# The state as stationary operand for z and n in a GRU with expert tiles

## What is computed

```python
def cell(h, x):
    gi = x @ W_ih + b_ih
    gh = h @ W_hh + b_hh
    r = sigmoid(i_r + h_r)
    z = sigmoid(i_z + h_z)
    n = tanh(i_n + r * h_n)
    return (1 - z) * n + z * h
...
y = sum over e of w[e] * ((silu(s @ W1[e].T) * (s @ W2[e].T)) @ W3[e].T)   # s: the states
x = x + y
```

## Time and profile before

| | us |
|---|---|
| median of 3 runs (1501.98 to 1507.65) | 1506.52 |
| span of the profiled execution | 1501.1 |
| TensorE matmul busy | 1409.4 (94%) |
| VectorE busy | 1043.8 (70%) |
| ScalarE busy | 896.3 (60%) |
| GpSimd busy | 415.8 (28%) |

### The profile page before, as it was taken

How to read it: one execution, slowest core, us unless ns; L and a number is a source line. 1 busy time by engine, 2 the same in 40 slices (tenths; PEclk the granted TensorE clock), 3 DMA queues, 4 the chain that set the end, 5 groups by cost and what they waited for, 6 DMA issues and landing times.

```text
span 1501.1 us, 88729 instructions
## 1 busy us (share of the span) xinstructions
PE 1409.4 (94%) x37804; PEld 1227.2 (82%) x37804; DVE 1043.8 (70%) x4116; ACT 896.3 (60%) x2319; POOL 415.8 (28%) x850
## 2 busy tenths in 40 slices
PE   2888878899999999999999999999999999998997
PEld 1888778888888888888888888888888888885664
DVE  7788887777677677777777767776777776764333
ACT  6677675555565556655556555665556655555664
POOL 1011112123322232222332223222333222326443
PEclk9999887899999999999999999999999999999999
DMA  8445413112221222212222122211222212223431
GB/s 290 124 130 140 134 45 90 40 32 40 46 39 39 46 46 40 39 39 46 40 46 40 39 46 46 41 38 40 46 40 46 40 39 47 39 40 79 60 49 16
DMA packets 99011, 88.64 MB, mean 59 GB/s; under 512 B 41407, under 2 KB 74175, under 8 KB 98624
## 3 DMA queue, kind: packets, MB, share of 16 engines
q0 software_dynamic: 17952, 33.64, 12.9%
q1 hardware_dynamic: 80672, 49.32, 11.5%
HBM read 59.12 MB, written 35.72 MB: 63 GB/s over the span
## 4 chain that ended last, share of the span: by engine, by line
PE 83%; DVE 10%; issue 3%; ACT 1%; POOL 1%; DMA 1%; SPq 0%; DVEq 0%; POOLq 0%; ACTq 0%
PE gn_bank L1366 12%; PE gz_ps L1366 12%; PE y_ps L1458 9%; PE b_ps L1388 9%; PE a_ps L1422 8%; PE b_ps L1422 8%; PE gi_ps L1388 8%; PE gr_ps L1357 6%; PE gr_ps L1351 6%; DVE wexp L1037 2%; PE tr_ps L1436 2%; PE tr_ps L1446 2%; PE tr_ps L1478 1%; DVE npre L1067 1%; DVE nmh L1073 1%
## 5 line engine op out<-in xcount | busy, mean ns | idle before, releaser
L1366 PE MATMUL gz_ps<-hlog,whh 128*128 128x32 f16 x8192 | 246.0, 177 | 6.1 <-issue 6.0
L1366 PE MATMUL gn_bank<-hlog,whh 128*128 128x32 f16 x8192 | 245.2, 177 | 2.4 <-issue 2.2
L625 POOL DMA_INDIRECT out_y<-work,mt x57 | 93.9, 1648 | 546.2 <-PE gz_ps L1366 309.6
L1366 PEld LDWEIGHTS gz_ps<-hlog,whh 128*128 128x128 f16 x8192 | 224.1, 96 | 6.9 <-issue 6.7
L1366 PEld LDWEIGHTS gn_bank<-hlog,whh 128*128 128x128 f16 x8192 | 224.2, 96 | 2.7 <-issue 2.7
L1351 PEld LDWEIGHTS gr_ps<-hlog,whh 128*128 128x128 f16 x4096 | 130.6, 96 | 53.9 <-DVE hlog L1080 32.4
L1351 PE MATMUL gr_ps<-hlog,whh 128*128 128x16 f16 x4096 | 141.9, 170 | 31.3 <-DVE hlog L1080 28.3
L1388 PE MATMUL b_ps<-xs,wih 128*128 128x64 f16 x4752 | 162.3, 197 | 3.4 <-issue 2.1
L1458 PE MATMUL y_ps<-wexp,work 128*128 x639 | 159.0, 382 | 1.9 <-ACT work L845 1.9
L1388 PEld LDWEIGHTS b_ps<-xs,wih 128*128 128x128 f16 x4752 | 153.3, 101 | 5.1 <-issue 3.5
L810 ACT ACTIVATE rs<-rpre,sc 128x64 f32<-128x64 f32 x256 | 88.0, 344 | 112.7 <-DVE rpre L1054 112.5
(11 more groups left out here) (217 smaller groups left out, 2550.3 us busy)
## 6 DMA issues: line engine op xcount, KB each, us to landing
wexp<-in_w_units SPq DMA_DIRECT2D x46, 256.0 KB, 3.8
x_raw<-in_x_feat SPq DMA_DIRECT2D x32, 256.0 KB, 3.7
out_y<-in_x_tok SPq DMA_DIRECT2D x16, 512.0 KB
h_tok<-xrow SPq DMA_DIRECT2D x32, 256.0 KB, 2.0
wexp<-in_w_hh SPq DMA_DIRECT2D x4, 768.0 KB, 6.8
wexp<-in_w_inproj SPq DMA_DIRECT2D x4, 768.0 KB, 11.8
wexp<-in_w_units SPq DMA_DIRECT2D x15, 192.0 KB, 4.5
mt<-meta SPq DMA_DIRECT2D x71, 1.0 KB, 1.7
```

The lines of the kernel that those rows point to most:

```text
L625: pool.indirect_dma_start(out=out, out_offset=bass.IndirectOffsetOnAxis(ap=mt[:, j % RING, 0:1].bitcast(I32), axis=0), in_=ysc[y_slot(j)], ...
L1366: mm = pe.matmul(dst[:, j], whh[:, i, k, m * P:(m + 1) * P], h[:, k], start=False, stop=True, skip_group_check=True)
```

## The change

For z and n the operands change places. The state of one chunk with both halves (128 x 32) is the stationary operand, and the weights stream past, 256 columns at a time: 8 blocks (4 of z, 4 of n) of 32 outputs. Four such matmuls, g = 0 to 3, use the four groups of 32 array columns and write to the four groups of 32 partitions of one bank, `zn_bank`; eight rounds (4 chunks, 2 halves of the weights) add up. So there are 32 matmuls in place of 64, z and n are finished together, and `gh_ready` counts two per step. r is made as before.

The results now lie with sequence and half on the partitions, in blocks of 32 x 32. VectorE turns each block back with a transpose of 32 x 32 (`turn`, one for n and one for z, from the bank to `n_parts` and `z_parts`), each followed by a sum over three numbers: the two halves and the bias or input part, which stands in the third place. For n that is written once in the setup; for z ScalarE writes it for each step (`place_z`), in place of the seed. The n seed goes. `hlog` has the two halves next to each other, so that its 32 columns are contiguous. The buffers `rs`, `zs`, `rh`, `nt` and `znh` go, and their operations write in place.

```diff
+    Q = 2 * B
-    GRU = "R HN R_HN N_PRE Z N_H Z_NH H_HI H_NEW H_LO".split()
+    GRU = "R N_TURNED HN R_HN N_PRE Z_TURNED Z N_H Z_NH H_HI H_NEW H_LO".split()
 ...
     def behind_n(t):
-        return 3 * t + 2
+        return 2 * t + 2
 ...
-        hlog = sb("hlog", [P, 2, K, 2, P], F16)
+        hlog = sb("hlog", [P, 2, K, P, 2], F16)
 ...
+        n_parts = sb("n_parts", [P, K, B, 3])
+        z_parts = sb("z_parts", [P, K, B, 3])
 ...
-        gn_bank = ps("gn_bank", [P, 512])
-        gn_ps = gn_bank[:, 0:K * 2 * B].rearrange("p (k a b) -> p k a b", k=K, a=2)
-        gz_ps = ps("gz_ps", [P, K, 2, B])
+        zn_bank = ps("zn_bank", [P, 512])
+        z_ps, n_ps = (zn_bank[:, i * K * 2 * B:(i + 1) * K * 2 * B].rearrange("p (k b a) -> p k b a", k=K, a=2)
+                      for i in range(2))
 ...
+            def place_z(t):
+                S.activation(z_parts[:, :, :, 2], gi_of(t, 1), ACT.Copy, scale=scale(SC_PLACE)).then_inc(z_placed, 1)
 ...
-                act.wait_ge(gru_ops, gru(t, "HN"))
-                if t + 1 < T:
-                    seed(gn_ps, bhn[:], n_seeded)
 ...
-                dve.wait_ge(gh_ready, 3 * t + 2)
-                halves(hn[:], gn_ps)
+                dve.wait_ge(gh_ready, 2 * t + 2)
+                turn(n_parts, n_ps)
+                after("N_TURNED")
+                total(hn[:], n_parts[:])
 ...
-                dve.wait_ge(gh_ready, 3 * t + 3)
-                halves(zpre[:], gz_ps)
+                turn(z_parts, z_ps)
+                dve.wait_ge(z_placed, t + 1)
+                after("Z_TURNED")
+                total(zpre[:], z_parts[:])
 ...
-                for dst, first, seeded in ((gn_ps, 2 * K, n_seeded), (gz_ps, K, z_seeded)):
-                    pe.wait_ge(seeded, t + 1)
-                    for j in range(K):
-                        m = first + j
-                        for k in range(K):
-                            for i in range(2):
-                                mm = pe.matmul(dst[:, j], whh[:, i, k, m * P:(m + 1) * P], h[:, k],
-                                               start=False, stop=True, skip_group_check=True)
-                    mm.then_inc(gh_ready, 1)
+
+                for k in range(K):
+                    for i in range(2):
+                        w = whh[:, i, k, K * P:M * P].rearrange("p (m x) -> p m x", x=P)
+                        for g in range(P // Q):
+                            mm = pe.matmul(zn_bank[g * Q:(g + 1) * Q, 0:4 * K * B], h[:, k].rearrange("p b a -> p (b a)"),
+                                           w[:, :, g * Q:(g + 1) * Q],
+                                           start=(k == 0 and i == 0), stop=(k == K - 1 and i == 1))
+                mm.then_inc(gh_ready, 1)
```

More of the change, by code:

```diff
@@ L54, in gru_moe_kernel @@
     assert GS == 8 and E == 8 and HE == 352 and TILES == 71 and FULL == 57
+    Q = 2 * B
+    assert Q == 32 and P // Q == K
     FIRST = 52
@@ L448, in h_parts @@
             g, s = divmod(t, GS)
-            return hlog[:, g % 2, :, :, s * B:(s + 1) * B]
+            return hlog[:, g % 2, :, s * B:(s + 1) * B]
         def raw_in(e, w):
@@ L903, in _ @@
             act.wait_ge(gates_open, 1)
-            seed(gr_ps, gi_of(0, 0), r_seeded)
-            seed(gn_ps, bhn[:], n_seeded)
-            seed(gz_ps, gi_of(0, 1), z_seeded)
+            seed_r(0)
+            place_z(0)
             for t in range(T):
@@ L933, in _ @@
                 if t + 1 < T and z_comes_late(t + 1):
-                    seed(gz_ps, gi_of(t + 1, 1), z_seeded)
+                    place_z(t + 1)
             take_rows(LAST)
@@ L1051, in op, with total, turn @@
                     ins.then_inc(gru_ops, 1)
[L1053 to L1057, removed]
+                def total(dst, parts):
+                    op(V.tensor_reduce(dst, parts, AX_X, ALU.add))
+                def turn(parts, rows):
+                    op(V.transpose(parts[:, :, :, 0:2], rows))
+                dve.wait_ge(gh_ready, 2 * t + 1)
+                total(rpre[:], gr_ps[:].rearrange("p k a b -> p k b a"))
                 behind_r(t)
-                dve.wait_ge(gh_ready, 3 * t + 2)
-                halves(hn[:], gn_ps)
+                dve.wait_ge(gh_ready, 2 * t + 2)
+                turn(n_parts, n_ps)
+                after("N_TURNED")
+                total(hn[:], n_parts[:])
                 dve.wait_ge(sig_r, t + 1)
                 after("HN")
-                op(V.tensor_tensor(rh[:], rs[:], hn[:], ALU.mult))
+                op(V.tensor_tensor(hn[:], rpre[:], hn[:], ALU.mult))
                 after("R_HN")
@@ L1076, in gru_step @@
                 after("N_H")
-                op(V.tensor_tensor(znh[:], zs[:], nmh[:], ALU.mult))
+                op(V.tensor_tensor(nmh[:], zpre[:], nmh[:], ALU.mult))
                 after("Z_NH")
-                for dst in (parts[:, :, 0], h_now[:, new]):
-                    op(V.tensor_tensor(dst, h_now[:, now], znh[:], ALU.add))
+                for dst in (parts[:, :, :, 0], h_now[:, new]):
+                    op(V.tensor_tensor(dst, h_now[:, now], nmh[:], ALU.add))
                 after("H_NEW")
-                op(V.tensor_tensor(parts[:, :, 1], h_now[:, new], parts[:, :, 0], ALU.subtract))
+                op(V.tensor_tensor(parts[:, :, :, 1], h_now[:, new], parts[:, :, :, 0], ALU.subtract))
             def expert_measure(e):
@@ L1265, in _ @@
             first = h_parts(2 * GS - 1)
-            chain(V.tensor_copy(first[:, :, 0], h_now[:, 0]))
-            chain(V.tensor_tensor(first[:, :, 1], h_now[:, 0], first[:, :, 0], ALU.subtract))
+            chain(V.tensor_copy(first[:, :, :, 0], h_now[:, 0]))
+            chain(V.tensor_tensor(first[:, :, :, 1], h_now[:, 0], first[:, :, :, 0], ALU.subtract))
             chain(V.tensor_scalar(scale(SC_GAP), scale(SC_PG), 2.0 ** -14, scale(SC_IH), ALU.mult, ALU.mult))
@@ L1477, in turn_rows @@
                         at = (i * K + k) * P
-                        mm = pe.transpose(tr_ps[:, at:at + P], h[:, k, i], ident[:])
+                        mm = pe.transpose(tr_ps[:, at:at + P], h[:, k, :, i], ident[:])
                 mm.then_inc(tr_mm, 1)
@@ L1481, in turn_rows @@
                     for k in range(K):
[L1482 removed]
+                        mm = pe.matmul(route_ps(g)[:, 0:2 * E], h[:, k, :, i],
                                        wg[:, k].rearrange("p e h -> p (e h)"),
@@ L1545, in _ @@
             pe.wait_ge(setup, N_CONSTS)
-            for gh in (gr_ps, gn_ps, gz_ps):
-                mm = pe.matmul(gh[:].rearrange("p k a b -> p (k a b)"), ident[:], ident[:], start=True, stop=True)
-            mm.then_inc(gates_open, 1)
+            pe.matmul(gr_ps[:].rearrange("p k a b -> p (k a b)"), ident[:], ident[:], start=True, stop=True
+                      ).then_inc(gates_open, 1)
             turn_x_exponent(0)
```

47 lines of the change are left out of this document (21 added, 26 removed).

## The result

The change makes the kernel slower: 1566.88 us (median of 4 runs, 1565.73 to 1567.64) against 1506.82 us (4 runs on the same chip), a ratio of 1.040 with a 95% interval of 1.0382 to 1.0418. The forecast was 1560 us; the terms behind it did less well than the sum, because two misses of nearly the same size cancel.

A forecast was written before the change was run, and what follows sets the result against it. TensorE was taken to bound steps 52 to 255 and the recurrence steps 0 to 51. Middle stage -13, first stage +49 and clock +18 make +54 us on 1506.5, so 1560 us, range 1506 to 1632.

The forecast's parts named there:

- The middle stage: Steps 52 to 255, mostly TensorE-bound: forecast 0.06 us shorter each over 203 steps, -13 us.
- the first stage: Steps 0 to 51, paced by the recurrence: forecast 0.95 us longer each, +49 us, plus 18 for the clock.
- the loop: Recurrence from one start of r to the next, through z, n and VectorE's chain: forecast 5.05 us against 3.98.
- two changes of mode: On TensorE between r on the full array and the column groups, and back: forecast 0.15 us each.
- place 3: Middle-stage steps whose number modulo 8 is 3: forecast length 5.05 us.
- place 7: Middle-stage steps whose number modulo 8 is 7: forecast length 5.05 us.
- place 2: Middle-stage steps whose number modulo 8 is 2, forecast to stay TensorE's: 5.58 us, TensorE's work down 0.42.
- E: End of the last z and n matmul; from there to the next r 3.08 us were forecast.
- The clock: Steps 0 to 51: streaming matmuls take about 1.7 us at the lower clock, 40% of the stage, +18 us.
- The first: Rival: cheaper turns and free mode change shorten the loop to 4.50, break even at 4.82; 1438 us, chance 0.10.
- The second: Rival: the four column groups run one after another, loop 7.66, about 2210 us; chance 0.10 together with the third.
- the third: Rival: weight loads don't hide, 8 rounds take 1.62 us, loop 5.79, about 1750 us; chance 0.10 together with the second.

The follow-up runs named there:

- e3: Changed kernel with all four matmuls of a round on the same 32 array columns, values not the reference's: 2197.6 us in one run.
- e4: Changed kernel with VectorE making the scale of hidden before the input-product batch in every fourth step: 1553.11 us, 1.029 of the kernel before.
- e5: Kernel before with one wait moved, so VectorE takes n only when z is finished too: 1531.48 us, ratio 1.0142.
- e9: Kernel before with an unread transpose ahead of each of the sums of n and z: 1527.06 us, ratio 1.0166.
- e6: Changed kernel with six unread matmuls of 512 columns a step in steps 0 to 49: 1558.51 us, 1.0322 of the kernel before.
- e7: Changed kernel with one transpose for n and z, hidden scale before input products, and the added clock-keeping matmuls: 1483.13 us, 0.9834 of the kernel before.
- e8: Kernel before with only the state's two halves laid side by side, read with doubled stride: 1507.39 us, ratio 0.9997.
- e1: Changed kernel with one transpose of 256 elements for n and z in place of two of 128: 1496.68 us, 0.9924 of the kernel before.
- e10: Changed kernel with z before n in two banks, z turned while n runs, hidden scale before input products: 1579.13 us, 1.0504 of the kernel before.
- e2: Changed kernel with n before z in two banks, 64 matmuls of 128 columns in place of 32 of 256: 1524.86 us, 1.011 of the kernel before.

## Why the prediction was right, and where not

**The sum: partly luck.** The terms were -13 + 49 + 18 = 54 us, and 60 came. The middle stage was forecast 29.5 us too low and the first stage 26 too high, and these cancel. 6.4 us more of the measured span lie before and behind the two stages. What was right without luck is the loop, and that it decides.

**The loop: right.** The 8 rounds follow each other 110 ns apart, 0.88 us in all as forecast, and z and n end 1.06 after their first start (forecast 1.03). The four groups run side by side (e3 shows the other case), starting 3 ns apart. The loads of 32 columns hide: each takes 100 ns, and the rounds take no longer than one stream does in e3 (109). The Trainium skill, TensorEngine Tiling (Array Packing), Restrictions, says that column tiling disables Fast Weight Load; the trace shows no time lost to that here. The two changes of mode take about 0.10 (r to z and n: 0.89 where r lasts 0.79 before) and 0.11 (0.99 from their first start to the next work, less 0.88), 0.21 in all against 0.30. From the start of r to the end of z and n it is 1.97 us in the waiting step (719.73 to 721.70), forecast 1.97. The Trainium skill, TensorEngine Tiling (Array Packing), Key Properties, says that a change of tiling mode drains the engine; a gap of this size agrees, though no run separates it from other causes. The first turn holds VectorE for 0.35 us until the sum (0.40 charged), the second for 0.41 (0.40).

**The middle stage: mis-sized, -13 forecast, +16.5 measured.** Eight steps at the forecast lengths make 40.93 us; at the measured medians 42.11. The difference is 1.18, of which place 3 has 0.57, place 7 has 0.52, place 2 has 0.11, and the rest cancels. 1.18 / 8 x 203 is 30 us, the whole miss. The step that failed is the sentence that VectorE's other work "fit on average in its gap of 1.6 us before E". The average held: VectorE is busy 4.31 us a step (875.88 / 203), 4.4 forecast. Two places out of eight didn't, since batch, scale and choice of experts are lumped. The prediction had even written down the price ("a turn starts late by the excess") and not taken it. At place 3 the turn itself is late by 0.63; at place 7 ScalarE is late with r's sigmoid, which the prediction didn't consider at all, and e4 shows that one by moving a single block (-0.53 at place 7, -14 us). At place 2, TensorE's step fell by 0.32 and not 0.42: from the first z and n matmul to the next work are 1.18 there in place of 0.99, and nothing shows why.

**The first stage: over-sized, +49 + 18 forecast, +40.8 measured.** On the kernel before, the lost cover alone gives +17.4 (e5) and the turns alone +19.3 (e9), 36.7 together; the granted clock fell in these runs too, from 0.87 to 0.83 and 0.84, and that they add up independently is not shown. Of e5's 0.80 us of later n only 17.4 / 52 = 0.33 a step was felt. In 39 of the 52 steps of the kernel before VectorE comes to n more than 0.1 us after its end, on average over all 52 by 0.54, and what it comes late by hides as much of the wait. Subtracted step by step from the 0.80, that leaves 0.38 (an estimate from these two), close to the 0.33. The prediction saw such steps ("one in which VectorE comes late") and priced them too near the waiting case: 0.84 us each, 0.95 on average.

**The clock: the mechanism is there, its price stays open.** The stage's granted clock fell from 0.87 to 0.81, the longer matmuls sum to 18 us, as forecast, and they are the streams of 256 columns that double (rounds 213 ns apart against 110). e6 and e7 don't measure what that costs, since the matmuls that hold the clock up delay r themselves. Where they don't, in 15 steps of e6, four fifths of the matmuls' gain reached the step (7.9 of 10.1 us). Taken for all of the 18 us that would be an estimate of 14 to 15.

**At nothing:** for the layout that was right (e8). Nothing in the middle stage fell to the lower clock (1.00).

**The rivals.** The first needed a loop under 4.82; the changed kernel's is 5.01. But e1 reaches it, at 4.76 to 4.86 in four of its eight places, and its 1496.68 us is 11 below the kernel before it on the same chip: the break even was placed about right. The second did not happen (e3 is what it would look like), nor the third: the rounds are 110 ns apart, not 203.

So why is it slower? TensorE gave back 0.32 us where it stayed the bound (place 2), and that kind of gain shows at places 1, 2, 5 and 6 (-0.45, -0.32, -0.17, -0.27). The recurrence became 1 us longer, and the other four places rose by 0.23 to 0.62. By these medians the middle stage gained 1.21 in eight steps and lost 1.92. The first stage, with little TensorE work to hide the longer loop, paid 41 us, two thirds of the loss.

What stays open: what the lower clock costs, as no run keeps it up without delaying r; and whether place 3 can be freed by spreading the choice of experts over two steps, which wasn't tried.

## What to carry to other kernels

When a change frees the busiest engine and lengthens a recurrence, compare the two step by step, not by averages: an average gap that holds the average work still overflows in the steps where the work is lumped. In such a chain the count of dependent operations matters more than their elements (one turn of 256 against two of 128 was worth 70 us), and work moved into a gap must be shorter than the gap (e10). A run that takes one cost away by added work has to be read for what the added work costs: e6's small gain looked like a cheap clock, and the added matmuls stood on the chain.

## What the hardware showed that was not expected

Full-array matmuls of 16 and 32 columns start 25 ns apart. Four matmuls in four groups of 32 array columns start 3 ns apart, and the next four follow 56 ns after the first four with 128 columns (e2) and 110 ns with 256 (the changed kernel). On the same array columns each one of 256 columns takes 109 ns (e3). So four such streams take the time of one, and 25 ns is not the least that lies between two matmuls.

A weight load of 32 columns takes as long as one of 128 (100 ns against 96), and four of them hide behind a round, even behind one of 56 ns, which is half a round of 256 columns.

VectorE's turn of 128 elements a partition from PSUM takes 316 ns, of 256 elements 448: about 1 ns for each further element, as its sums have.

At the lower clock (granted 0.50 around 245.87) the group of 32 takes 1.90 us against 1.06, while the short matmuls of n before took 0.85 against 0.80.
